# A conv-attention, linear-attention and MoE block on one core: weights merged earlier, and the residual turned into the experts' accumulators

## The reference

```python
h = group_norm(x, 32 groups) * scale + bias
q, k, v = h @ Wq + bq, h @ Wk + bk, h @ Wv + bv
x = x + softmax(q k^T / sqrt(C)) v @ Wp + bp              # 1024 x 1024 per batch
t = tokens(x)                                             # 4 x 1024 tokens of 128
n = layernorm(t); q, k, v = n @ W_qkv                     # 4 heads of 32
t = t + ((softmax_over_tokens(k)^T v) applied to q*scale) @ W_out + b_out
n = layernorm(t); p = softmax(n @ router^T); keep the two largest, normalised
t = t + n + sum_e share[:, e] * (gelu(n @ w1[e] + b1[e]) @ w2[e] + b2[e])   # 8 experts
return channels_first(t)
```

## Time and profile before

| what | us |
|---|---|
| runs of the kernel | 324.09, 322.27, 324.42 (median 324.09) |
| the profiled execution | 323.33 |
| its span | 321.6 |
| TensorE busy | 298.4 (93%) |
| VectorE busy | 255.3 (79%) |
| ScalarE busy | 200.2 (62%) |
| GpSimd busy | 155.7 (48%) |
| experts' phase | 193 to 319 |

### The profile page before, as it was taken

The page is one execution under the profiler, slowest core; times in us unless marked ns, Lnnn a source line. Parts: engine busy times, 40 slices in busy tenths (PEclk is TensorE's granted clock), DMA queues, the critical chain, the costliest instruction groups (busy, mean ns, idle before and its releaser), DMA issues.

```text
span 321.6 us, 5478 instructions
## 1 busy us (share of the span) xinstructions
PE 298.4 (93%) x1574; PEld 237.3 (74%) x1574; DVE 255.3 (79%) x637; ACT 200.2 (62%) x348; POOL 155.7 (48%) x358
## 2 busy tenths in 40 slices
PE   2998989989999999999999997997989998999895
PEld 2877868866878887888886886875758776568684
DVE  4599686596587797987698975998698895799895
ACT  3257374568670695762487674676677654878782
POOL 2859793059932974960984100899540059000000
PEclk9999999999999999999999999999999999999999
DMA  5901000010000021000000138485310692249501
GB/s 142 323 4 68 0 1 2 0 65 2 1 3 0 0 67 66 2 12 0 0 1 10 55 94 263 175 347 185 150 67 1 206 371 108 73 190 374 185 1 65
DMA packets 12760, 29.61 MB, mean 92 GB/s; under 512 B 2192, under 2 KB 5952, under 8 KB 10816
## 3 DMA queue, kind: packets, MB, share of 16 engines
q1 hardware_dynamic: 12448, 29.00, 25.8%
q10 hardware_dynamic: 288, 0.33, 0.3%
HBM read 24.73 MB, written 4.59 MB: 91 GB/s over the span
## 4 chain that ended last, share of the span: by engine, by line
PE 52%; DVE 20%; POOL 9%; issue 6%; DMA 5%; ACT 4%; SPq 1%; DVEq 0%; POOLq 0%; ACTq 0%
PE ring L1433 10%; PE ring L1418 6%; PE ring L1420 6%; PE ring L1419 6%; PE scores L1418 5%; PE scores L1420 5%; PE scores L1419 4%; DVE prob L1033 4%; POOL w_n L577 3%; DVE pT_lo L1040 3%; POOL u L577 2%; DMA cb_in<-scratch_c 2%; POOL rstd L572 2%; PE ring L1578 2%; PE ring L1556 2%
## 5 line engine op out<-in xcount | busy, mean ns | idle before, releaser
L840 ACT ACTIVATE gel<-scores,b_c 128x512 f32<-128x512 f32 x64 | 43.7, 686 | 22.8 <-PE scores L1420 22.1
L568 POOL TENSOR_SCALAR rstd<-lmv 128x4 f32<-128x4 f32 x16 | 4.5, 283 | 89.3 <-DVE lmv L1075 88.0
L1040 DVE TENSOR_TENSOR pT_lo<-ring,pT_hi 128x512 fp32r<-128x512 f32 x64 | 40.4, 680 | 7.2 <-ACT pT_hi L704 7.1
L698 ACT ACTIVATE prob<-prob,row_max 128x1024 f32<-128x1024 f32 x32 | 36.8, 1149 | 13.4 <-DVE prob L1033 13.4
L1033 DVE TENSOR_SCALAR_CACHE_REDUCE prob<-scores 128x1024 f32<-128x1024 f32 x32 | 38.6, 1213 | 3.3 <-PE scores L1420 3.3
L704 ACT ACTIVATE pT_hi<-ring 128x512 fp32r<-128x512 f32 x64 | 34.6, 598 | 9.4 <-PE ring L1433 9.1
L1433 PE MATMUL ring<-ident,prob 128*128 128x128 f32 x256 | 33.6, 275 | 2.3 <-ACT prob L698 1.5
L1433 PEld LDWEIGHTS ring<-ident,prob 128*128 128x128 f32 x256 | 28.7, 140 | 7.0 <-ACT prob L698 2.3
L1418 PE MATMUL scores<-wT_hi,w_hi 128*128 128x512 f32 x64 | 30.4, 475 | 0.0
L1418 PE MATMUL scores<-k_both,q_hi 128*128 128x512 f32 x64 | 27.1, 423 | 0.6 <-DVE prob L1033 0.6
L1418 PE MATMUL ring<-pT_hi,v_hi 128*128 128x512 f32 x64 | 26.6, 415 | 0.8 <-DVE pT_lo L1040 0.8
(11 more groups left out here) (297 smaller groups left out, 775.4 us busy)
## 6 DMA issues: line engine op xcount, KB each, us to landing
pT_hi<-scratch_s SPq DMA_DIRECT2D x8, 1024.0 KB, 6.3
prob<-scratch_s SPq DMA_DIRECT2D x4, 1024.0 KB, 7.8
k_both<-scratch_s SPq DMA_DIRECT2D x3, 1024.0 KB, 6.3
z_in<-scratch_z SPq DMA_DIRECT2D x8, 256.0 KB, 3.0
out_dram<-out_s SPq DMA_DIRECT2D x8, 256.0 KB, 2.2
xb<-in_x_dram SPq DMA_DIRECT2D x3, 512.0 KB, 3.3
scratch_z<-out_s SPq DMA_DIRECT2D x2, 512.0 KB, 2.8
k_both<-scratch_s SPq DMA_DIRECT2D x4, 256.0 KB, 4.7
```

The lines of the kernel that those rows point to most:

```text
L698: act.activation(prob[:, i % 2, :], prob[:, i % 2, :], ACT.Exp, bias=row_max[:, i:i + 1], scale=-1.0, accum_out=row_sum[:, 0, i:i + 1]).th ...
L840: act.activation(half(gel, s % 2), scores[:, s % 2, :], ACT.Gelu, bias=b1_c[:, s % E:s % E + 1]).then_inc(e_gelu, 1)
L1040: dve.tensor_tensor(tile_group(pT_lo, n, i), as_tiles(ps(place, unit)), tile_group(pT_hi, n, i).bitcast(FP32), ALU.subtract).then_inc(drai ...
```

## The change

Three things are changed together.

*The merge.* wvT, wpv and bias_o are made by TensorE in the group-norm stage, ahead of q0, and l1qT right behind the first biases. They use banks 4 and 5, of the scores. ScalarE copies them (take, output_bias) instead of VectorE. keep_busy is called in other places: four products at once when the constants are there, then one at a time between the group's means, its variances and the merge. The order of VectorE's opening changes too.

*The residual.* turn_z, its copies by ScalarE and its store are gone. SyncE stores the tokens t2 as they are, to scratch_t, and loads them as t_in. In outward, at e = 0, TensorE turns the four tiles of t_in straight into the accumulator, with is_transpose, and the experts' products add to that. The b2 product, and with it the wait for cb_in, moves from e = 0 to e = 7. result becomes ScalarE's copy of the accumulator. GpSimd's add_bout waits for the store of the tokens (t_stored) where it waited for the turn z1.

*The lists.* z goes from all tables. Of batch 2, o and st come at step 2 instead of 0 and lg at 15 instead of 12; of batch 3, most pieces come one step earlier. Banks in the opening change, row_maximum(4) of a loop batch comes behind two turns of probabilities, and WHOLE keeps sixteen steps, but in part other ones.

```diff
-SETUP_UNITS = dict(gn_mean=0, gn_var=1, bias_qk=2)
+SETUP_UNITS = dict(gn_mean=0, gn_var=1, bias_qk=2, wvT=4, wpv=5, bias_o=4, l1qT=5)
...
-TAIL_AT = dict(m3=0, PV=0, o=0, st=0, OT=5, OTst=6, w0=9, w1=9, lg=12, u0=14, u1=14, lT=16, rA=17, kT=20, exp=20, rB=20, ks=23, z=17, p=21, rC=20, g=23, c=24)
-END_AT = dict(ctx=24, m2=26, m3=28, o=29, st=29, w0=36, w1=36, lg=37, lT=38, rA=38, exp=38, rB=38, rC=39, z=41, c=41)
+TAIL_AT = dict(m3=0, PV=0, o=2, st=2, OT=5, OTst=6, w0=9, w1=9, lg=15, u0=14, u1=14, lT=16, rA=17, kT=20, exp=20, rB=20, ks=23, p=21, rC=20, g=23, c=24)
+END_AT = dict(ctx=24, m2=25, m3=27, o=28, st=28, w0=35, w1=35, lg=36, lT=37, rA=37, exp=37, rB=37, rC=38, c=41)
...
-WHOLE = frozenset((4, 6, 12, 15, 16, 22, 26, 29, 31, 33, 34, 35, 36, 37, 38, 40))
+WHOLE = frozenset((4, 6, 16, 18, 19, 20, 22, 24, 28, 30, 32, 33, 34, 35, 37, 40))
...
+            def store_tokens(lc):
+                sp.wait_ge(z_made, lc + 1)
+                apart(sp)
+                sp.dma_start(scratch_t[bass.ds(lc, 1)].rearrange("a p t -> (a p) t"),
+                             t2[:, :, :].rearrange("p j c -> p (j c)")).then_inc(t_stored, 16)
...
-                sp.dma_start(half(z_in, h), scratch_z[m * HALVES + h]).then_inc(z_loaded[h], 16)
+                sp.dma_start(half(t_in, h), half(scratch_t[m], h)).then_inc(t_loaded[h], 16)
...
             def add_bout(lb, routed):
-                if routed is not None:
-
-                    wait_filled(pool, routed, "z1")
+                if routed:
+
+                    pool.wait_ge(t_stored, lb * 16 + 16)
+                    apart(pool)
...
             split_first()
+            take("wvT", wvT[:, :])
+            take("wpv", wpv[:, :])
+            act.wait_ge(ld_w["cols"], 64)
+            output_bias()
+            take("l1qT", l1qT[:, :])
             opening_batch(FIRST, SECOND, 0)
...
+            def result(m, h):
+                place = y_place(m)
+                act.wait_ge(e_y, m * (2 * E) + (h + 1) * E)
+                if not first_batch(m):
+                    act.wait_ge(stored[h], m * 16)
+                act.activation(half(out_s, h), ps(place, f"y{h}"), ACT.Copy).then_inc(drained[place.bank(f"y{h}")], 1)
...
-                dve.tensor_tensor(half(out_s, h), ps(place, f"y{h}"), half(z_in, h), ALU.add
-                                  ).then_inc(drained[place.bank(f"y{h}")], 1)
...
                 project(place, b, "q0", q_hi, q_lo, bq_c)
+                group_stats(1)
                 project(place, b, "k0", k_hi, k_lo, bk_c)
                 project(place, b, "k1", k_hi, k_lo, bk_c)
-                take(place, "wvT", wvT[:, :])
-                group_stats(1)
+                group_stats(2)
+                row_maximum(place, b, 0)
                 project(place, b, "q1", q_hi, q_lo, bq_c)
-                row_maximum(place, b, 0)
-                merge_weights()
                 row_maximum(place, b, 1)
-                group_stats(2)
                 project_v(place, b)
...
+            def merge_values():
+
+                pe.wait_ge(ld_w["wv"], 16)
+                turn(SETUP, "wvT", [wv_s[:, :]])
+                keep_busy(1)
+                wait_drained(pe, SETUP, "wvT")
+                pe.wait_ge(ld_w["wp"], 16)
+                small(SETUP, "wpv", C, wvT[:, :], wp_s[:, :])
+                pe.wait_ge(ld_w["cols"], 64)
+                small(SETUP, "bias_o", 1, wp_s[:, :], bv_c)
...
             pe.wait_ge(const_made, 1)
+            keep_busy(4)
             group_means(SETUP, 0, 0, 1)
             keep_busy(1)
             group_variances(SETUP, 0, 0, 1)
-            keep_busy(4)
+            merge_values()
+            keep_busy(1)
...
                 if e == 0:
                     open_unit(place, f"y{h}")
+                    pe.wait_ge(t_loaded[h], m * 16 + 16)
+                    for j in range(QUAD):
+                        pe.matmul(tile(dst, j), tile(half(t_in, h), j), ident[:, :], start=j == 0, stop=False,
+                                  is_transpose=True)
+                if e == E - 1:
                     pe.wait_ge(c_loaded[h], m * 32 + 32)
-                    pe.matmul(dst, b2_parts[:, :], cb_in[:, h, :], start=True, stop=False)
+                    pe.matmul(dst, b2_parts[:, :], cb_in[:, h, :], start=False, stop=False)
```

More of the change, by code:

```diff
@@ L230, in conv_attention_moe @@
         comb = sb("comb", [P, 2, P])
-        gel, hs, hw, out_s, z_in = (sb(n, [C, T]) for n in ("gel", "hs", "hw", "out_s", "z_in"))
+        gel, hs, hw, out_s, t_in = (sb(n, [C, T]) for n in ("gel", "hs", "hw", "out_s", "t_in"))
         cb_in = sb("cb_in", [P, HALVES, BANK], FP32R)
@@ L244, in conv_attention_moe @@
         x_of = [xb, gel, hs, out_s]
-        zT_early, cT_early = out_s[:, :], (z_in[0:TILES * E, 0:P], z_in[:, P:2 * P])
-        zT_late = xb[:, :]
+        cT_early = (t_in[0:TILES * E, 0:P], t_in[:, P:2 * P])
         cT_late = (xT[0:TILES * E, 0, :], xT[:, 1, :])
@@ L653, in batch @@
                 first_norm(la)
-                add_bout(la, place if lc is not None else None)
+                add_bout(la, lc is not None)
             batch(SECOND, 1, 0, None)
@@ L749, in route_exp @@
                 act.activation(rt[:, 1, :, :], rt[:, 0, :, :], ACT.Exp).then_inc(r_exp, 1)
-            def turn_z(place, lc, zT):
-                act.wait_ge(z_stored, lc * 16 + 16)
-                for n in range(HALVES):
-                    unit = f"z{n}"
-                    wait_filled(act, place, unit)
-                    act.activation(half(zT, n), ps(place, unit), ACT.Copy).then_inc(drained[place.bank(unit)], 1)
             def w_halves(lb):
@@ L859, in experts @@
                         high(m - 1, 2 * E - 1)
+                    if s == LAG and not first_batch(m):
+                        result(m - 1, 1)
+                    if s == E + LAG:
+                        result(m, 0)
                     between_steps(between, m, s)
@@ L1602, in turn_logits @@
                 fill(place, "lT", last)
-            def turn_z(place, lb):
-                pe.wait_ge(z_made, lb + 1)
-                for n in range(HALVES):
-                    turn(place, f"z{n}", tiles_of(t2, n))
             def turn_comb(place, lb):
@@ L1619, in opening_batch @@
                 project(place, b, "q1", wq_hi, wq_lo)
-                pe.wait_ge(ld_w["wv"], 16)
-                turn(place, "wvT", [wv_s[:, :]])
                 for unit in ("q0", "k0"):
@@ L1624, in opening_batch @@
                 score(b, 0, lambda: wait_drained(pe, place, "k1"))
-                wait_drained(pe, place, "wvT")
-                pe.wait_ge(ld_w["wp"], 16)
-                small(place, "wpv", C, wvT[:, :], wp_s[:, :])
-                pe.wait_ge(ld_w["cols"], 64)
-                small(place, "bias_o", 1, wp_s[:, :], bv_c)
+                wait_drained(pe, SETUP, "bias_o")
+                wait_drained(pe, SETUP, "l1qT")
                 score(b, 1)
-                wait_drained(pe, place, "wpv")
+                wait_drained(pe, SETUP, "wpv")
                 pe.wait_ge(h_f_made, 1)
@@ L1635, in opening_batch @@
                 score(b, 2)
-                pe.wait_ge(ld_w["qkv"], 16)
-                turn(place, "l1qT", [wqkv_s[:, 0:C]])
                 pe.wait_ge(ld_w["rows8"], 32)
```

87 lines of the change are left out of this document (34 added, 53 removed).

## The result

The changed kernel runs in 321.24 us (median of 20), the kernel before in 323.23 (median of 20). The ratio of the runs is 0.9931, 95% interval 0.9906 to 0.9956: 0.7% faster, 2.2 us. It leaves out the slow executions (324.68 and 324.80 of the changed kernel), so it comes out a little above the 2.0 between the two medians. The two profiled executions differ by more, 323.33 to 319.70, in span 321.6 to 317.7. Why these are not the same number is the main thing the experiments had to find.

The account below looks back on a forecast made before the run. TensorE was taken as the bound, busy 93% of the span with 52% of the chain. Opening -2.4, batches 2 and 3 -0.9 and experts -0.6 made -3.9 against 323.33, so 319.4 us; range 316.6 to 322.8.

Parts of the forecast that it names:

- within 1%: Outcome case for the whole kernel: measured time less than 1%, 3.2 us, from no change; chance 0.33.
- R2: Rival, experts: the wait at step 14 costs the clock, price 3.0 to 4.9 us, or 8 or more if repeated; chance 0.10.
- Opening, -2.4: Opening: merge, lost VectorE copies and an earlier clock rise save 2.4 us, between ends of 1.2 and 3.1.
- Batches 2 and 3, -0.9: Batches 2 and 3: without z, ScalarE's next pT_hi comes earlier, giving VectorE about 0.45 per batch, 0.9 us saved.
- Statistics at step 2, +0.9: Experts: take_out and statistics at step 2 reach GpSimd later, so u's second half starts 0.9 us later.
- Logits behind the wait, +0.9: Experts: four logits products move from ahead of the wait for u to behind it, costing 0.9 us.
- p, end lists, -0.6 and -0.6: Experts: the wait for p gives back 0.6 us; end lists one step earlier bring statistics and w_n 0.6 earlier.
- cb_in and t_in, -1.1: Late experts: the 1.15 wait for cb_in goes and t_in, issued 0.9 earlier, lands in time; 1.1 us saved.
- R5: Rival, late experts: the queue keeps the wait, t_in lands late and nearly all of 1.1 goes; 320.2 us, chance 0.08.
- R1: Rival, opening: the clock rises where it did, so the opening gives only 1.2; 320.6 us, chance 0.13.
- R3: Rival, experts: turns into an accumulator cost 0.22 instead of 0.11 each, +1.75 us; 321.5 us, chance 0.10.
- R4: Rival, experts: the wait for u doesn't grow; 318.2 us, or 317.3 with a quicker u; chance 0.14.

Follow-up runs that it names:

- before_fill: Kernel before the change, with 6 dummy products ahead of TensorE's wait for cb_in; 324.54 us, ratio 1.0022 to the kernel before.
- no_first_busy: Changed kernel without keep_busy(4), its first four dummy products at 3 us; 322.11 us, ratio 0.9918 to the kernel before.
- rowmax_back: Changed kernel with row_maximum(4) of batches 2 and 3 ahead of two turns of probabilities again; 321.56 us, ratio 0.9946 to the kernel before.
- stats_back: Changed kernel with VectorE's group_stats(1) and (2) and split of q1 at their old places; 321.83 us, ratio 0.9946 to the kernel before.
- out_step0: Changed kernel with batch 2's attention output and its statistics (o, st) back at step 0 instead of 2; 321.80 us.
- lg12: Changed kernel with the logits of batch 2 back at step 12, ahead of u's turns; 319.78 us, ratio 0.9861 to the kernel before.
- t_early: Changed kernel loading t_in of the last batch's first half ahead of the shares; 319.65 us, ratio 0.986 to the kernel before.
- fill_u: Changed kernel with 8 and 4 dummy products ahead of the two halves of u's turns; 319.54 us, ratio 0.986 to the kernel before.
- old_lists: Changed kernel with the old step tables (without z) and row_maximum(4) at its old place; 320.82 us, ratio 0.9931 to the kernel before.
- merge_only: Kernel before the change plus only the weight merge, its banks and VectorE's opening order; 323.33 us, ratio 0.9975 to the kernel before.
- after_again: The changed kernel, unedited, run again beside the kernel before; 321.76 us over 12 executions, ratio 0.9954.

## Why the prediction was right, and which of its steps failed

The time, 319.4 forecast and 321.24 measured, lay in the range, and the forecast of a gain held. By the prediction's own line at 320.9, though, it fell in the case "within 1%", which had 0.33, not in "faster", which had 0.62. The sum of -3.9 is nearly that of the profiled pair (-3.6), and that is in part luck: at the last product the opening has given 1.6 of 2.4, batches 2 and 3 1.8 of 0.9, and the experts 0.4 of 0.6, so two misses cancel. What separates 319.7 from 321.2 is rival R2, which I had given 0.10. The statement that the ends span 317.4 to 321.3 is no plain sum either: the three ends as listed add up to 316.0 and 322.7.

- **Opening, -2.4.** Measured 1.6 where the pace came late in both (61.66 to 60.05), and 0.3 where it came at 11.6 in the list of before (before_fill). The failed step is that with full pace at 9.41 the scores start 3 earlier. The early record did nothing for the clock (no_first_busy), and the scores could not start earlier, since I had left the 1.28 of group_stats(1), moved ahead of the k splits, out of the chain to the scores (rowmax_back: full pace at 11.9, scores at 15.71, behind a wait of 1.79 for k_both). Over eleven traces with the new order, with full pace anywhere from 11.9 to 16.3, batch 1's q0 starts between 44.2 and 44.8: the changed opening no longer hangs on the clock, that of before does by 1.3. What was right is that the order and the lost copies pay without any help from the clock: I had 1.2, and where the pace came late in both it is 1.6, of which the order is 0.9 (stats_back's batch 1 turn stands at 60.99).
- **Batches 2 and 3, -0.9.** Measured -1.8, 2.3 with the wait for m: the product ahead of m starts at 194.52 and 191.12, 3.4 apart, where 1.6 was had. My 0.45 per batch for z is what came (12.70 to 12.19). The failed step is one that I costed at nothing without naming a cover: row_maximum(4). Ahead of it TensorE waited 0.39 for pT_lo in each batch. rowmax_back shows the wait and 0.76.
- **Statistics at step 2, +0.9.** Failed. I priced the later take_out at a whole 0.9 for GpSimd; its first row came 3.31 earlier where TensorE's product with m was 3.94 ahead, so it was 0.6 later against TensorE, but w_n started 4.2 earlier and u's second half was ready 4.05 earlier. out_step0 is slower, not faster. That GpSimd gets no quicker beside the experts held (u took 8.30).
- **Logits behind the wait, +0.9.** Right: lg12, 1.1 at 1.0. The wait grew from 2.0 to 3.0 (in two parts), not to 4, for want of the 0.9 above.
- **p, end lists, -0.6 and -0.6.** Right in sum. Between steps 18 and 42 the lead grows by 1.0 (4.07 to 5.04), although there twelve turns of t_in come and only eight of z go, about 0.4 against it. But the parts are others: the wait for p went whole, 0.98, and w_n's hardly changed, 1.30 instead of 1.41.
- **cb_in and t_in, -1.1.** Mis-sized: 0.99 of the 1.15 stayed. The failed step is that a load issued earlier lands as much earlier. TensorE needed it 4.5 earlier (298.66 to 294.13) and it was issued 5.9 earlier, but it landed in 10.3 instead of 8.7, since its landing hangs on the shares ahead of it, 4.1 earlier. t_early, which takes it out from behind them, removes the wait. So R5, the queue keeps the wait, was true, though not for a late issue.
- **R2.** Place right, price lower (1.3 at 0.995, 2.8 at 0.989; I had 3.0 and more), chance far too low: 25 of 31 executions lost clock, with waits of 1.96 and 1.06 and not with one of 4. Both traces of the changed kernel kept the clock, so that it fell here rests on fill_u (6 of 6 at 1.0) and on the traces of out_step0, no_first_busy and t_early. In these the products behind step 14 start 0.43 apart, which the prediction had named as a sign of being wrong. The Trainium skill, "TensorE: Matmul & The Clock Gate", "HAM oscillation — how this bites in real kernels", was on the right side: waits between bursts, if long enough, bring the clock down and the next burst starts slow. The rows of out_step0 agree (0.50 behind waits of 2.01 and 1.06), and fill_u shows that it is the waits.
- **R1** was true in its mechanism: the dummies did not bring the clock. **R3** was wrong: 0.60 for four turns. **R4** was half true: the wait grew by 1.0 and not by 1.8, but u got no quicker (8.30).

Open: where the kernel before loses its clock (0.995 in 35 of 77 executions). Its wait of 2.0 for u was not filled; against that place speaks old_lists, which kept its clock in 11 of 11 executions with a wait of 1.81 for u, and for the wait for cb_in speaks merge_only's trace. Open too: where the second fall of the executions at 0.989 lies, and why no_first_busy is slower at 0.995.

## What to carry to other kernels

When a list is changed, look at the waits it leaves on TensorE also for their length and neighbours: idle time that costs nothing by itself can cost the clock of the products behind it, and dummy products that fit in the wait can give it back. A single profiled execution can miss this; compare medians of runs at equal granted clock. Price moves of instructions on the engine that leads, even those that look like housekeeping: here the place of one row maximum was worth 0.38 a batch, where eight removed turns gave 0.5. And before issuing a load earlier, look at what lies ahead of it in its queue.

## What the runs showed of the hardware

- TensorE's mean granted clock takes few values over a run, nearly always 1.0, 0.995 or 0.989. One fall in a trace is about 3.4 us at 1.2 GHz (221.35 to 224.8 in out_step0), which is 0.005 of 320 us, and 0.989 would be two, though no trace caught both. From level to level the changed kernel loses 1.3 and 1.5 us, the kernel before 1.8 and 2.6.
- It fell behind waits of 1.9 to 2.0 and 1.1 with four turns between them (out_step0, no_first_busy, t_early), and behind single waits of 2.43 (merge_only) and 2.83 (rowmax_back, for t_in; 0.50 from 298 to 301), but not behind every one: the traces of after_again, rowmax_back, stats_back and the changed kernel have the first pair of waits without the fall.
- The half pace of the opening isn't in the page's granted clock, which reads 1.0 there; it ends at any time from 11.6 to 16.3 us in fourteen traces, at 13.1 in the only one of a changed opening without the first four dummies and at 11.6 and 15.5 in the two with the opening of before.
- A load of 256 KB landed in 2.7 us when issued 8.7 ahead of 3 MB of broadcast shares (t_early) and in 8.7 to 10.6 behind them, 12.3 to 13.3 after the first of them was issued in eleven of twelve traces.
